# Self-attention of a decoder layer: TensorE takes the values of step s - 3 ahead of the scores of step s, not behind them

## What is computed

```python
logits = jnp.einsum('bihd,bjhd->bhij', q, k) * scale + pos_bias[None]
attn = jax.nn.softmax(logits, axis=-1)
out = jnp.einsum('bhij,bjhd->bihd', attn, v).reshape(B, S, D)
...
x = _layernorm(x + _L0_attn_ref(x, ...), axis=-1)
```

## Time and profile before

| what | us |
|---|---|
| median of 3 runs | 1478.68 (1477.83 to 1479.94) |
| the profiled execution, its own time | 1476.96 |
| its span, first to last instruction | 1475.2 |
| self-attention in it, first scores to last copy | 143.4 to 656.9 |
| mean granted TensorE clock | 0.943 |

### The profile page before, as it was taken

The page is one execution under the profiler, slowest core; times in us unless marked ns, Lnnn a source line. Parts: engine busy times, 40 slices in busy tenths (PEclk is TensorE's granted clock), DMA queues, the critical chain, the costliest instruction groups (busy, mean ns, idle before and its releaser), DMA issues. The chain is left out here.

```text
span 1475.2 us, 19316 instructions
## 1 busy us (share of the span) xinstructions
PE 1354.6 (92%) x6462; PEld 621.9 (42%) x6462; DVE 856.6 (58%) x1244; ACT 811.4 (55%) x991; POOL 662.8 (45%) x461
## 2 busy tenths in 40 slices
PE   8987999999999999976999972998999999999966
PEld 3533222222222222213555541854666666666645
DVE  3534788888888888862454544582344343343326
ACT  4544899999999999972565630002222222222236
POOL 2222677777777777753434311202333333333313
PEclk9998899999999999997999985599999999999988
DMA  6598345574495544423222006902111111111137
GB/s 212 162 351 242 138 81 88 90 229 66 65 243 85 85 75 70 69 69 101 74 66 63 1 0 198 389 27 65 47 45 45 47 46 44 47 48 43 47 124 236
DMA packets 107238, 155.72 MB, mean 106 GB/s; under 512 B 27649, under 2 KB 72102, under 8 KB 106598
## 3 DMA queue, kind: packets, MB, share of 16 engines
q1 hardware_dynamic: 100208, 135.79, 35.1%
q0 software_dynamic: 6816, 18.62, 4.0%
q10 hardware_dynamic: 118, 0.05, 0.0%
HBM read 110.65 MB, written 43.78 MB: 105 GB/s over the span
## 5 line engine op out<-in xcount | busy, mean ns | idle before, releaser
L669 DVE TENSOR_TENSOR sa_probs<-sa_sum,sa_strips 128x1024 f32<-128x1024 f32 x352 | 413.4, 1219 | 74.3 <-PE sa_sum L624 70.2
L711 POOL TENSOR_TENSOR sa_probs<-sa_probs,sa_factors 128x1024 f32<-128x1024 f32 x160 | 381.1, 2382 | 134.5 <-ACT sa_probs L687 134.5
L693 ACT ACTIVATE sa_probs<-sa_probs 128x1024 f32<-128x1024 f32 (+1 forms) x256 | 341.2, 1374 | 0.3 <-DVE sa_probs L669 0.3
L638 PE MATMUL sa_o<-sa_probs,sa_v 128*17 128x512 f32 x2048 | 270.6, 600 | 1.1 <-POOL sa_probs L711 0.6
L1985 PE MATMUL xp_ps_h<-w,arena 128*128 x568 | 257.2, 596 | 1.2 <-ACT arena L2039 1.1
L2039 ACT ACTIVATE arena<-xp_ps_x 128x256 f32<-128x256 f32 x71 | 27.2, 383 | 375.7 <-PE xp_ps_x L1977 375.7
L624 PE MATMUL sa_sum<-sa_q,sa_k 97*128 97x512 bf16 x704 | 199.2, 387 | 6.2 <-PEq L127 4.4
L2078 DVE TENSOR_TENSOR arena<-xp_ps_h,ffn_b 128x1024 f32<-128x1024 f32 x71 | 87.0, 1225 | 195.1 <-PE xp_ps_h L1985 195.1
L687 ACT ACTIVATE sa_probs<-sa_factor 128x1024 f32<-128x1024 f32 x160 | 163.2, 1020 | 29.3 <-PE sa_factor L624 29.3
L624 PEld LDWEIGHTS sa_sum<-sa_q,sa_k 97*128 97x128 bf16 x704 | 48.5, 98 | 251.6 <-DVE sa_probs L669 195.5
L1985 PEld LDWEIGHTS xp_ps_h<-w,arena 128*128 128x128 f32 x568 | 108.3, 191 | 108.5 <-issue 104.9
(11 more groups left out here) (223 smaller groups left out, 1443.5 us busy)
## 6 DMA issues: line engine op xcount, KB each, us to landing
sa_q<-qstack SPq DMA_DIRECT2D x96, 128.0 KB
sa_k<-kstack SPq DMA_DIRECT2D x96, 128.0 KB
sa_strips<-line SPq DMA_DIRECT2D x3, 3840.0 KB, 15.7
oT<-sa_o_out SPq DMA_DIRECT2D x32, 256.0 KB, 2.3
co_y<-y_places SPq DMA_DIRECT2D x16, 512.0 KB, 8.8
kstack<-qp_parts SPq DMA_DIRECT2D x48, 128.0 KB, 3.7
qstack<-qp_parts SPq DMA_DIRECT2D x48, 128.0 KB
sa_factors<-factor_line SPq DMA_DIRECT2D x3, 1920.0 KB, 19.8
```

Of the source, the lines that this page charges most:

```text
L638: last = nc.tensor.matmul(ps_o[n % 2][32 * h:32 * h + VW, :], v[m % 2][:, jt, VW * h:VW * (h + 1)], probs[s % RING][:, h, :], start=(jt == ...
L669: nc.vector.tensor_tensor(probs[s % RING][:, 2 * half:2 * half + 2, :], ps_sum[sums_before(s, half) % 2][:, :, :], strips[hg % 2][:, 2 * h ...
L693: nc.scalar.activation(probs[s % RING][:, 0:heads, :], probs[s % RING][:, 0:heads, :], ACT.Exp, scale=0.25).then_inc(exp_done, 1)
L711: nc.gpsimd.tensor_tensor(probs[s % RING][:, 2:4, :], probs[s % RING][:, 2:4, :], factors[hg % 2][:, :, c1 - CH:c1][:, :, ::-1], ALU.mult) ...
```

## The change

Two lines of TensorE's loop change places. No instruction is added or removed, and the programs of the other four engines are the same row for row.

```diff
@@ -640,10 +640,10 @@
                 last.then_inc(pv_done, 1)
 
             for s in range(NSTEP + LAG):
+                if s >= LAG:
+                    values(s - LAG)
                 if s < NSTEP:
                     scores(s)
-                if s >= LAG:
-                    values(s - LAG)
```

## The result

The changed kernel takes 1570.28 us (median of 4 runs, 1568.52 to 1571.48) and the kernel before 1478.26 (4 runs, 1474.98 to 1479.94): ratio 1.0624, 95% interval 1.0603 to 1.0646. It is 92 us slower; 94 were forecast.

What follows compares the result with a forecast made beforehand. The prediction took TensorE to bound the self-attention. It added 93.8 us for the steady part, 0.5 for the start and 0 for the end, about 94, to 1476.96, and said 1572 us, 8 in 10 within 1555 to 1598.

Steps and rivals of the forecast that it cites:

- TensorE is the bound and a stop is paid in full: Self-attention: matmuls busy 463.70 of 465 us, waiting 0.3 us, so anything that stops TensorE costs its full time.
- The lag has 1 us to spare at jt 1, 4 and 7: V there starts about 1 us after E ends; moved 1.97 us earlier, it would be 0.97 or 0.98 late.
- The ring of seven links: V(1), S(4), V(2), S(5), F(5), E(4), V(4), likewise V(4) to V(7): three steps take 6.92 us, 5.90 before.
- the short one: V(7) through S(2), F(2) and E(1) to the next group's V(1): two steps take 4.92 us, 3.94 before.
- Eight steps 18.76 for 15.75: Steady part: 6.92 + 6.92 + 4.92 us, 3.0 more per eight steps; 31.25 groups from S(5) to S(255) give 93.8.
- The start costs 0.5: Before S(5), at 1.2 GHz, one V more stands on TensorE: 0.5 us, with 0 and 1.8 as ends.
- The end costs nothing: From S(255) over A(255) and E(255) to V(255) the way is the same in both orders: 0 us.
- The factor steps' stops are covered by the others: V(3) waits for W(3), about 0.4 us late, but the stop at V(1) just before already moves its place by 0.97.
- The clock is costed at nothing: Self-attention clock stays at 1.00 with TensorE 84% busy; the rival that it falls at times had chance 0.11.
- The last sum: Whole kernel: 1476.96 + 94 = 1571, plus 1.7 for the median, said as 1572; likeliest case 1566 to 1583.
- The hidden: Rival: TensorE runs scores while a V waits, or E and W come a step sooner: 1476 to 1480 us, chance 0.03.
- the faster rival: Rival: V moved ahead gives VectorE's A the 0.05 us waits back, 4.8 us: about 1474 us, chance 0.02.

Runs made afterwards that it cites:

- Experiment 2: A 128-element exponential added on ScalarE between F(s+1) and E(s) at jt 1, 4, 7: changed kernel 1592.75 us, kernel before 1479.09 us.
- experiment 3: Changed kernel with E of jt 1, 4 and 7 split in halves, the first ahead of F(s+1), the second behind: 1494.68 us.
- experiment 8: Kernel before with E of jt 1, 4 and 7 split in halves around F: 1478.82 us, ratio 1.0002.
- experiments 1 to 4: First of these: changed kernel with GpSimd's W over one of its two heads, 1574.18 us; the others have their own lines.
- Experiment 6: Kernel before with V moved ahead of the scores only for factor steps (jt 0, 2, 3, 5, 6): 1544.47 us, ratio 1.0444.
- experiment 4: Changed kernel with E of jt 1, 4 and 7 split in halves, both behind F(s+1): 1583.01 us, ratio 1.0695.

## Why the prediction was right

- *TensorE is the bound and a stop is paid in full.* Right: the self-attention takes 94.7 us more. The profile's idle time before V, 91.8 in sum, is not the price itself: 94 stops of 0.96 in the row of steps move V by 1.03 each, and 1.5 of the sum is one stop at the end, at V(255). V(1) of the first group, at 1.2 GHz, has no stop, so it is 95 for the 96 forecast.
- *The lag has 1 us to spare at jt 1, 4 and 7 and a step is 1.97, so V is 0.97 or 0.98 late.* Right that V is late at these places and, in the steady part, only there. The size in the steady part is not set by the spare time but by the ring, which gives 6.92 - 5.90 = 1.02 for two of the three stops and 0.98 for the third; that 0.97 comes so near is in part chance.
- *The ring of seven links, 6.92, and the short one, 4.92.* Right: 6.93 and 4.94, and each link within 0.01 or 0.02, but for V(5) to S(0) at the first scores of a batch row, 1.12 for 1.03 in both kernels. Experiment 2 lengthens a link and experiment 3 shortens one, and the time follows: 0.6 for 3 x 0.20 longer; for 3 x 0.85 shorter it is 2.56.
- *Eight steps 18.76 for 15.75.* The difference, 3.0, measured 3.04: both have on average 0.05 to 0.08 more than the eight steps I read, which almost cancels. The sum for S(5) to S(255) was 93.8 and is 95.1. The whole, 94.3 forecast, is 92.0 by the medians and 94.7 in the self-attention: 1.3 more here and 0.8 less at the start nearly cancel, and the rest is the scatter of the other stages. So the total is met within 3 us in part by luck.
- *The start costs 0.5.* Off, in a small term: it gave 0.3 back, just below the ends of 0 and 1.8. The granted clock is 0.50 there in both kernels, but it is back at 1.00 by 154 us after and by 156 before. S(4) took 1.89 us at 153.22 before; now, in TensorE's timeline, it runs in 1.04:

```profile
154.21 1.04 PE L624 MATMUL sa_sum<-sa_q,sa_k 97*128 97x512 bf16 x4
```

  The changed order isn't needed for that. In experiment 2's kernel before, whose TensorE has the old order and whose first scores stand at 146.56, S(4) runs at the full clock too:

```profile
156.41 1.04 PE L625 MATMUL sa_sum<-sa_q,sa_k 97*128 97x512 bf16 x4
```

  From the first scores to S(5) the old order takes 12.97, 11.85 (this kernel) and 13.46 us (experiment 8), the changed one 12.63, and 12.85, 12.63, 12.54 and 11.50 in experiments 1 to 4. In the three of the old order the clock comes back 12.4, 9.9 and 13.4 us behind the first scores. So the moment of its rise moves this stretch by more than 0.5 or -0.3, and these runs cannot tell the term from nothing.
- *The end costs nothing.* Right, 6.87 for 6.88.
- *The factor steps' stops are covered by the others.* Right in the changed kernel: no stop stands at a factor step, but for 0.47 us at V(254), which waited 0.56 for W before. Experiment 6 shows what that sentence must not be read as: moved alone, they cost 65 us by another way.
- *The clock is costed at nothing.* Right in its result, 1.00 in the stage. But its evidence was thin: the stretch from 80 to 100 us, at 1.00 in the kernel before, is at 0.83 in the profile after, although nothing was changed there (windows view):

```profile
80.00:100.00 20.00, 17.23 (x42) 8.07 (x41) 6.45 (x12) 7.55 (x15) 5.73 (x5) 0.83 1.06 373
```

- *The last sum.* 1478.68 + 94.3 is 1573, not 1572, and 90 to 104 on top of that median is 1569 to 1583, not from 1566. Nothing hangs on it.
- *The hidden and the faster rival.* Both out by the 87 stops. The page TensorE: Matmul & The Clock Gate of the Trainium skill, cited for the clock, tells of pauses that make the clock swing; here pauses of 0.96 us, three in 18.8 us for 600 us, left it at 1.00.

## What to carry to other kernels

When one engine's program takes a consumer one place earlier, read the spare time of each consumer (its start less the end of what it waits for) and set it against a whole step. Where it is smaller, follow what stands behind the waiting instruction on every engine until the way comes back to it: the sum of that ring is the new time of those steps. Idle time of an engine inside the ring is no room for work that is put on the ring's way (experiment 2, behind F); it is room only for work that can be done before what the engine waits for (experiment 3, half of E ahead of F). If a ring binds, take work off it by splitting an instruction so that the part whose input is early goes ahead of the one that the ring passes through; changing the two round as a whole can just move the stop to the next engine.

## What the runs showed of the hardware beyond that

- Groups of eight alternate between 15.84 and 15.74 us before, and 18.88 and 18.78 after. The 0.1 stands at the first scores of a batch row, which follow V by 1.12 us and not 1.03 (444.62 to 445.74 above). There TensorE has one more semaphore to wait for (the loads of q, k and v, long landed). But a further wait, already met, does not cost that everywhere: V of jt 0 also has one more (for the copy of sa_o two groups before) and stands 0.97 behind the scores like the others. These scores are also the first to read the other buffers of q and k. So the cause of the 0.09 us is open. In experiment 6, where these scores wait for VectorE anyway, the alternation is gone (17.92 and 17.93).
- ScalarE's instructions over 128, 1024 and 2048 elements a row take 0.30, 1.05 (F, which reads sa_factor, 1.02) and 1.90 us, and the next one starts about 0.1 us ahead of the end of the one before. The Trainium skill, page ScalarE: Activation LUTs, section What ACT_TABLE_LOAD costs, gives a fixed part of 186 ns and 0.833 ns for each element, with an overlap of 93 ns; the rows agree within 0.02 us. So the split of E costs 0.1 each time, as experiment 4 shows.
